# A perceiver block on one core: two feed-forward output tiles made together, matmul by matmul in turn into two PSUM banks

## What is computed

```python
h1 = gelu(einsum('th,ehf->etf', nx, up_W) + up_b)
s0 = gelu(ln(einsum('etf,efg->etg', h1[0], spec0_W) + spec0_b))
t1 = gelu(einsum('etf,efg->etg', h1[1], spec1a_W) + spec1a_b)
s1 = ln(einsum('etg,egf->etf', t1, spec1b_W) + spec1b_b)
s2 = gelu(einsum('etf,efg->etg', h1[2], spec2_W) + spec2_b)
y += einsum('eth,te->th', einsum('etf,efh->eth', h2, down_W) + down_b, w)
```

## Time and profile before

| what | value |
|---|---|
| median of 3 executions | 2820.15 us (2812.32 to 2821.58) |
| the profiled execution's own time | 2822.73 us |
| its span | 2820.8 us |
| TensorE matmul busy | 2772.0 us (98%) |
| VectorE busy | 1510.4 us (54%) |
| ScalarE busy | 1465.7 us (52%) |
| mean granted TensorE clock, share of 2.4 GHz | 0.997 |
| feed-forward part in the span | 1907 to 2821 us |

### The profile page before, as it was taken

The page is one execution under the profiler, slowest core; times in us unless marked ns, Lnnn a source line. Parts: engine busy times, 40 slices in busy tenths (PEclk is TensorE's granted clock), DMA queues, the critical chain, the costliest instruction groups (busy, mean ns, idle before and its releaser), DMA issues.

```text
span 2820.8 us, 68080 instructions
## 1 busy us (share of the span) xinstructions
PE 2772.0 (98%) x27742; PEld 2280.1 (81%) x27742; DVE 1510.4 (54%) x2283; ACT 1465.7 (52%) x1341; POOL 878.2 (31%) x621
## 2 busy tenths in 40 slices
PE   7999999999999999999999999989999999999999
PEld 6777777777777777777777777749999998999998
DVE  5444444444444444444444444556488565567754
ACT  3545555555555555555555545536456475546554
POOL 5445454444545444444545444410000000000000
PEclk9999999999999999999999999999999999999999
DMA  5433333333333332333333333314544555545553
GB/s 175 112 109 83 84 89 79 92 82 92 80 87 86 81 89 81 92 83 90 81 86 88 79 89 81 83 59 157 191 176 168 193 189 190 192 178 192 180 193 127
DMA packets 196505, 334.53 MB, mean 119 GB/s; under 512 B 22088, under 2 KB 122568, under 8 KB 175312
## 3 DMA queue, kind: packets, MB, share of 16 engines
q1 hardware_dynamic: 196432, 333.50, 38.9%
HBM read 281.50 MB, written 51.90 MB: 118 GB/s over the span
## 4 chain that ended last, share of the span: by engine, by line
PE 55%; issue 17%; DVE 8%; DMA 6%; POOL 5%; SPq 2%; ACT 1%; DVEq 0%; POOLq 0%; ACTq 0%
PE f_ps L1606 24%; PE kv_ps L1257 16%; PE y_ps L1590 5%; PE kv_ps L1313 5%; PE s_ps L1302 4%; DMA k_rows<-k_dram 4%; POOL ctx_lo L507 3%; DMA k_dram<-k_blocks 2%; DVE k_n L863 2%; POOL k_var L517 2%; SPq L410 2%; DVE k_blocks L867 1%; DVE ctx_hi L834 1%; DVE kt_hi L844 1%; PE mid_ps L1438 1%
## 5 line engine op out<-in xcount | busy, mean ns | idle before, releaser
L586 ACT ACTIVATE probs<-s_ps 128x3072 f32<-128x3072 f32 x260 | 711.6, 2737 | 807.0 <-PE s_ps L1302 518.2
L517 POOL TENSOR_TENSOR k_var<-k_var,neg_half 128x16 f32<-128x16 f32 x196 | 569.7, 2907 | 15.4
L507 POOL TENSOR_TENSOR ctx_lo<-ctx_raw,ctx_hi 128x512 fp32r<-128x512 f32 x196 | 253.2, 1292 | 920.3 <-DVE ctx_hi L834 749.9
L863 DVE TENSOR_TENSOR k_n<-k_centred,k_var 128x496 f32<-128x496 f32 x196 | 135.6, 692 | 642.5 <-issue 432.7
L789 DVE TENSOR_TENSOR w_lo<-w_raw,w_hi 128x2048 fp32r<-128x2048 f32 x160 | 367.3, 2296 | 176.7 <-ACT w_hi L643 176.6
L1606 PE MATMUL f_ps<-h_hi,w_hi 128*128 128x256 f32 x1536 | 430.7, 280 | 0.0
L1606 PE MATMUL f_ps<-h_hi,w_lo 128*128 128x256 f32 x1536 | 429.7, 280 | 0.0
L1606 PE MATMUL f_ps<-h_lo,w_hi 128*128 128x256 f32 x1536 | 429.7, 280 | 0.0
L1313 PE MATMUL kv_ps<-probs,v_sb 128*32 128x256 f32 x6272 | 353.8, 381 | 1.9 <-ACT probs L586 1.4
L643 ACT ACTIVATE w_hi<-w_raw 128x2048 fp32r<-128x2048 f32 x160 | 306.0, 1913 | 75.4 <-PE y_ps L1590 61.9
L1257 PE MATMUL kv_ps<-wk_hi,ctx_hi 128*128 128x496 f32 x784 | 324.5, 414 | 9.4 <-POOL ctx_lo L507 7.0
(11 more groups left out here) (215 smaller groups left out, 4607.5 us busy)
## 6 DMA issues: line engine op xcount, KB each, us to landing
w_raw<-w_dram SPq DMA_DIRECT2D x160, 1024.0 KB, 4.8
ctx_raw<-ctx_dram SPq DMA_DIRECT2D x196, 256.0 KB, 2.7
k_dram<-k_blocks SPq DMA_DIRECT2D x784, 64.0 KB, 1.8
k_rows<-k_dram SPq DMA_DIRECT2D x196, 256.0 KB, 3.0
qkv_w<-qkv_w_dram SPq DMA_DIRECT2D x12, 256.0 KB, 3.5
bias_rows<-bias_rows_dram SPq DMA_DIRECT2D x1, 1280.0 KB, 14.5
wq<-wq_dram SPq DMA_DIRECT2D x1, 1024.0 KB, 5.7
wk_rows<-wk_dram SPq DMA_DIRECT2D x1, 1024.0 KB, 7.7
```

The lines of the kernel that those rows point to most:

```text
L507: g.tensor_tensor(ctx_lo[r % 2][:], raw[r % 3][:], ctx_hi[r % 2][:].bitcast(f32), ALU.subtract).then_inc(ctx_lo_made, 1)
L517: g.tensor_tensor(k_var[:, 2], k_var[:, 1], neg_half[:].to_broadcast([P, H]), ALU.pow)\
L586: s.activation(probs[run][:], s_ps[:], ACT.Sigmoid).then_inc(probs_made, 1)
L863: v.tensor_tensor(k_n[:, :, 0:DR], k_c[:], per_row(k_var[:, 2], DR), ALU.mult)\
```

## The change

For layers with 4 or 2 tiles a chunk, TensorE takes two tiles at a time. It waits for both banks first, then goes through k and the three products and issues each product for the first tile and then for the second. Signals stay attached to each tile's own last matmul. Layers with one tile a chunk and down layers are issued as before. The numbers of matmuls, weight loads and signals stay the same.

```diff
-                            for j in range(per):
-                                n = i * per + j
-                                slot = n % 4
-
-                                pe.wait_ge(f_read, at(half, TILES_HALF, q, 4 * per, FILL_BASE[name] + n + 1))
+                            if per:
                                 hi, lo = (w[i][:].rearrange("p (k n) -> p k n", k=kt) for w in (w_hi, w_lo))
-                                cols = slice(j * P, (j + 1) * P)
+                            together = min(per, 2)
+                            for j in range(0, per, 2):
+                                for side in range(together):
+                                    pe.wait_ge(f_read, at(half, TILES_HALF, q, 4 * per,
+                                                          FILL_BASE[name] + i * per + j + side + 1))
                                 for k in range(kt):
                                     if i == 0 and j == 0:
                                         source(k)
                                     for m, (w, r) in enumerate(((hi, s_hi), (hi, s_lo), (lo, s_hi))):
-                                        ins = t.matmul(f_ps[:, slot, 0:TOK], w[:, k, cols], r[:, k],
-                                                       start=(k == 0 and m == 0),
-                                                       stop=(k == kt - 1 and m == 2))
-                                if j < per - 1:
-                                    ins.then_inc(f_made, 1)
+                                        for side in range(together):
+                                            ins = t.matmul(f_ps[:, (i * per + j + side) % 4, 0:TOK],
+                                                           w[:, k, (j + side) * P:(j + side + 1) * P], r[:, k],
+                                                           start=(k == 0 and m == 0),
+                                                           stop=(k == kt - 1 and m == 2))
+                                            if k == kt - 1 and m == 2 and j + side < per - 1:
+                                                ins.then_inc(f_made, 1)
                             ins.then_inc(w_used, 1)
```

## The result

In 14 executions each, the changed kernel took 2821.24 us in the median (2818.15 to 2826.20), the kernel before 2812.50 us (2807.62 to 2821.58; the first three of these are the ones shown above, and they lay high). The ratio of the comparison is 1.0024, 95% interval 1.0014 to 1.0034: 6.8 us slower, under the 0.3% bound, so no change by that measure, with a sign. By the three ratios the loss is 2 to 7 us.

What follows compares the result with a forecast made beforehand. TensorE, busy 98%, was taken to bound the kernel through matmul count times pitch. Terms of 0 + 0 + 0 + 1.4 + 0 gave 2824.1 us on the profiled execution, 2821.5 on the median; range 2806 to 2831.

Steps and rivals of the forecast that it cites:

- What bounds the kernel: Feed-forward part: time is matmul count times pitch, 113.4 or 117.8 ns, plus a few microseconds of waits; TensorE busy 98%.
- Step 1: Up layers and spec1b: changing the bank at each of 2,304 matmuls is worth 1.4 us at most either way; taken as 0.
- Step 2: Weight loads: each matmul already has its own load, so separating the two uses of high weights costs 0.
- Step 3: ScalarE's reads of finished tiles come in bursts; cover before TensorE needs the banks shrinks from 2.3 to 0.8 us, cost 0.
- rival B: Slower: a late burst of ScalarE reads stalls TensorE in up layers and may turn the pitch slow; 2826 to 2831, chance 0.10.
- Step 4: Existing stall in up2, both halves: tile 5 must now be read as well, 2 x 0.71 us, cost 1.4 us.
- Step 5: Waits of the first chunk get looser but gain 0; spec2 behind up2 still gets its input in time, cost 0.
- The sum: All terms together: 0 + 0 + 0 + 1.4 + 0 = +1.4 us, counted as no change.
- Rival A: Faster: alternating banks moves the stream into the quick pitch, 2815 to 2801.6 us, middle 2809; chance 0.17.
- cheap form: Two late chunks of w_raw at 1.3 us less 0.8 of cover, with the longer up2 stall: 2.5 us.
- dear part: One new stall in up0 of half two turns 1200 quick matmuls slow, 5.3 us; all quick ones, 8.4 us.

## Why the prediction was right, point by point

The forecast was no change, +1.4 us, range 2806 to 2831; measured were no change by the bound, 2821.24 us, and ratios that put the loss at 2 to 7 us. That 2821.5 came so near 2821.24 is partly luck: it was built on a median of three executions that lay 7.65 us over the median of fourteen. The difference forecast was 1.4 us, that of the first comparison is 6.8; what the traces show as the change's own is 2.0.

**What bounds the kernel**: right. In kernels of the same waits the length of the feed-forward part followed the pitches to within 0.2 us. The prediction misnames one row: the 192 in 22.62 us are the start of spec1b; the end of spec1a took 22.61 us, at the same pitch.

**Step 1** (a change of bank is worth nothing): right, and shown where it was argued. Paired matmuls, each into another bank than the one before, have 113.3 and 117.8 ns, to a tenth the numbers of matmuls that stay in one bank. No stretch of the tile line in any run came near the estimate of 109.2 ns; the quickest had 113.3.

**Step 2** (weight loads): right, by the same rows; the counts of loads and matmuls did not move.

**Step 3** (bursts of reads, cost 0): this is the term that failed, though by little. I worked the cover out in a steady chunk of up1, 0.8 us, and it held there. It did not hold at two places with something extra in ScalarE's queue. In up0 of the first half the gelu table's 1.28 us fell between a pair's end and its reads: 0.24 us idle, and with the longer starts around it 0.4 to 0.5 us lost. The kernel before loads this table in the same place, and step 3 left it out. In up1 of the second half w_hi waited 0.73 us for its chunk, as rival B had it:

```profile
2397.34 1.92 ACT L643 ACTIVATE w_hi<-w_raw 128x2048 fp32r<-128x2048 f32 x1 [0.73 <-DMA w_raw<-w_dram]
...
2400.23 0.48 ACT L758 ACTIVATE h_hi<-f_ps,bias_cols 128x256 fp32r<-128x256 f32 x1
```

That read ends at 2400.71, and TensorE's next pair starts at 2400.86, 0.33 us behind the last two starts in place of 0.23:

```profile
2400.53 0.39 PE L1607 MATMUL f_ps<-xn_hi,w_lo 128*128 128x256 f32 x2
2400.86 0.48 PE L1607 MATMUL f_ps<-xn_hi,w_hi 128*128 128x256 f32 x2
2401.17 0.28 PE L1607 MATMUL f_ps<-xn_lo,w_hi 128*128 128x256 f32 x1
```

The next two starts take 0.31 us, again more than 0.23: 0.2 us in all, in this profile alone of the three. The cover of 0.8 us was thus a little too large, since 0.73 us of lateness used it up. Together the misses of step 3 are 0.5 to 0.7 us.

**Step 4** (the stall in up2): right in place, cause and size, 2 x 0.72 us measured for 2 x 0.71. Pairs in up2 alone came out 1.5 us longer in the table's last column. The wait of the second half is itself 0.37 us behind slow matmuls and 0.79 behind quick ones; the pairs added 0.72 to either, 1.09 in the first profile of the changed kernel and 1.52 in the third.

**Step 5**: right; no wait for inputs at the start of spec2 or spec1b is in the trace after.

**The sum** was thus 1.4 us and should have been 1.9 to 2.1. The term of step 3, put at 0, measured 0.5 to 0.7.

**Rival A** (the alternation gives the quick pitch): wrong. Slow and quick stretches are found in paired layers as in others. (Its count of quick matmuls in the kernel before, 1,900, leaves out 144 of spec1a in the first half.)

**Rival B**: its mechanism appeared in up0 and once in up1, and cost 0.5 to 0.7 us; its cheap form had 1.1 us for it (2.5 less step 4's 1.4). Its dear part, a stall that turns the pitch, happened in up0 in four of the five profiles with a stall there, but for 190 matmuls only (0.8 us), because behind the router's matmuls the pitch was slow in every profile at this placement anyway; in the fifth the stall turned a slow pitch quick. The 910 matmuls behind the late chunk stayed quick.

**What stays open.** The ratios give losses of 6.8, 3.4 and 2.3 us, and the waits explain 2.0. What the rest is made of is not shown. One candidate is the draw of the pitch: behind each stall of up2 a draw decides over 864 matmuls, 3.8 us. With pairs in up2, 9 of 12 such stretches were slow in the profiles; without, 4 of 8. That is too few to say that the longer stall makes the slow pitch likelier; the run with pairs in up2 alone, which had both quick and no loss in its median, speaks against. The other is the part ahead, which the change does not touch: the feed-forward part began anywhere from 1902.2 to 1908.3 us in the fourteen profiles, so that it varies by nearly as much as the first loss.

## What to carry to other kernels

Before reordering matmuls to spare a bank, compare starts in the trace where the bank already changes with starts where it does not; here that answered the question to a tenth of a nanosecond before anything was built. Work that is handed over in pairs has half the cover and waits for the later of two: its price is at the places where the consumer's queue holds something extra (a table load, a late chunk, a long step of another engine), not in the steady state. And when two medians differ by less than their spread, subtract what varies by itself, here above all 4.44 ns for each slow matmul, and the change is readable in single profiles; a matmul ahead of a stall that another engine ends is not to be subtracted.

## What the runs showed of the hardware that was not expected

- **Two pitches for the same matmul.** The stream of weight load and 256-column matmul runs at 113.33 or 117.78 ns, at a granted clock of 1.00, holds it through hundreds of tile ends and signals, and takes one anew after an interruption: a stall, or matmuls of another kind. Some interruptions always gave the same (slow behind the router's matmuls, quick in the up layers that follow down2 and down3, in all ten profiles of this placement), others either. This alone moved the feed-forward part by up to 10.1 us (4,118 against 1,833 slow matmuls) between profiles. What picks one of the two was not found.
- **The place of the tiles in SBUF sets the pitch.** Moving the feed-forward tiles, which hold the moving operands, by 32, 64 and 96 bytes with the weight tiles left in place gave 118.3, 120.0, and 116.7 or 117.8 ns, and cost 0.60%, 0.85% and 0.36%. At 64 bytes the down layers' matmuls of 512 columns went the other way, 226.9 ns (43.57 us for 192) where the kernel before has 228.9. A 4-byte tile put in for an experiment did more harm than any edit of the order of work. Which pair of operands matters, and why, was not tried.
